# Latent attention: separate semaphores for the loads of QA and QB, and each query projected in slot 0 of a step

## What is computed

```python
B, T, C = (2, 512, 256); H, D = (16, 64); R = C // 8; ROPE = D // 2; NOPE = D - ROPE
q = (x @ Wq).reshape(b, t, H, D).transpose(0, 2, 1, 3)
ckv = x @ Wkva
kv_latent, k_rope = (ckv[:, :, :R], ckv[:, :, R:])
kv = (kv_latent @ Wkvb).reshape(b, t, H, NOPE).transpose(0, 2, 1, 3)
q = jnp.concatenate([q_nope, _rope(q_rope)], axis=-1)
k = jnp.concatenate([kv, _rope(k_rope)], axis=-1)
v = jnp.concatenate([kv, jnp.zeros_like(k_rope)], axis=-1)
att = jnp.einsum('bhqd,bhkd->bhqk', q, k) / jnp.sqrt(jnp.float32(D))
att = jax.nn.softmax(jnp.where(causal, att, -inf), axis=-1)
y = jnp.einsum('bhqk,bhkd->bhqd', att, v)
```

## Time and profile before

| what | value |
|---|---|
| median of 3 executions | 2580.61 us (2579.28 to 2582.89) |
| the profiled execution | 2586.34 us |
| its span (first to last instruction of the program) | 2584.6 us |
| stage of latent attention, steps 0 to 63 | 434.7 to 1490 us of the span |
| mean granted TensorE clock over the span | 0.965 |

### The profile page before, as it was taken

The page is one execution under the profiler, slowest core; times in us unless marked ns, Lnnn a source line. Parts: engine busy times, 40 slices in busy tenths (PEclk is TensorE's granted clock), DMA queues, the critical chain, the costliest instruction groups (busy, mean ns, idle before and its releaser), DMA issues. The chain is left out here.

```text
span 2584.6 us, 45266 instructions
## 1 busy us (share of the span) xinstructions
PE 2365.7 (92%) x16756; PEld 1955.3 (76%) x16756; DVE 1812.6 (70%) x3346; ACT 1340.9 (52%) x2031; POOL 930.2 (36%) x1042
## 2 busy tenths in 40 slices
PE   7998867999999999999999879999778888999999
PEld 5777655777777777777777768888667777888887
DVE  6888874787778777877787656666566657666564
ACT  5666543666666676667666643332234443333322
POOL 0323334364546464645444321121346641010000
PEclk8999987999999999999999979999889998999999
DMA  4011104433343334333433152332301113121221
GB/s 143 19 44 53 30 18 138 122 106 102 109 144 108 108 112 144 107 103 106 139 108 109 57 196 60 93 103 74 125 9 35 36 47 120 38 77 46 73 58 42
DMA packets 193179, 223.60 MB, mean 87 GB/s; under 512 B 37160, under 2 KB 156608, under 8 KB 189312
## 3 DMA queue, kind: packets, MB, share of 16 engines
q1 hardware_dynamic: 192960, 220.71, 29.3%
HBM read 150.75 MB, written 55.47 MB: 80 GB/s over the span
## 5 line engine op out<-in xcount | busy, mean ns | idle before, releaser
L1271 DVE TENSOR_REDUCE l_negmax<-l_mx 128x1 f32<-128x512 f32 (+3 forms) x608 | 390.8, 652 | 74.9 <-PE l_mx L1663 74.2
L1284 DVE TENSOR_TENSOR l_Plo<-l_s,l_Phi 128x512 fp32r<-128x512 f32 x576 | 368.8, 682 | 24.0 <-ACT l_s L1518 21.7
L1514 ACT ACTIVATE l_Phi<-l_s 128x1024 fp32r<-128x1024 f32 x288 | 293.7, 1020 | 136.3 <-PE l_s L1687 135.0
L1698 PE MATMUL l_o<-l_Phi,l_V 128*128 128x256 f32 x1152 | 301.6, 284 | 1.2 <-DVE l_Plo L1284 0.8
L1698 PE MATMUL l_o<-l_Plo,l_V 128*128 128x256 f32 x1152 | 299.4, 282 | 0.0
L1663 PE MATMUL l_mx<-l_KK,l_QA 128*128 128x512 f32 (+3 forms) x768 | 278.6, 402 | 20.7 <-DMA l_QB<-l_qd 11.2
L1518 ACT ACTIVATE l_s<-l_s 128x1024 f32<-128x1024 f32 x288 | 294.2, 1021 | 0.0
L2834 ACT ACTIVATE m_hidhi<-m_h 128x512 fp32r<-128x512 f32 x168 | 106.4, 633 | 355.5 <-DVE m_h L2683 355.5
L1685 PE MATMUL l_s<-l_QA,l_KK 128*128 128x512 f32 x576 | 257.6, 447 | 22.0 <-DVE l_Plo L1284 18.5
L1698 PEld LDWEIGHTS l_o<-l_Plo,l_V 128*128 128x128 f32 x1152 | 218.2, 189 | 16.1
L1687 PE MATMUL l_s<-l_QB,l_KL 65*128 65x512 f32 (+1 forms) x576 | 230.1, 399 | 0.0
(11 more groups left out here) (473 smaller groups left out, 6370.1 us busy)
## 6 DMA issues: line engine op xcount, KB each, us to landing
l_qd<-l_qs SPq DMA_DIRECT2D x256, 128.0 KB, 2.3
l_QA<-l_qd SPq DMA_DIRECT2D x64, 512.0 KB, 3.6
l_QB<-l_qd SPq DMA_DIRECT2D x64, 256.0 KB, 4.4
l_R<-l_rd SPq DMA_DIRECT2D x128, 128.0 KB, 2.9
m_spread<-m_combs SPq DMA_DIRECT2D x62, 256.0 KB, 5.2
m_spread<-m_combs SPq DMA_DIRECT2D x124, 128.0 KB, 4.9
xs<-next_store SPq DMA_DIRECT2D x32, 256.0 KB, 2.0
l_rps<-l_rp SPq DMA_DIRECT2D x128, 64.0 KB, 1.9
```

The source lines that it names most:

```text
L1271: v.tensor_reduce(negmax[:, n % 2, at + h0:at + h1], piece_of(number, chunk), AX.X, ALU.max, negate=True).then_inc(reduced, 1)
L1284: v.tensor_tensor(Plo[:, s % 3, x].rearrange("p h q -> p (h q)"), S2[s % 2][:, x * HALF:(x + 1) * HALF], Phi[:, s % 3, x].rearrange("p h q ...
L1514: a.activation(Phi[:, s % 3].rearrange("p u h q -> p (u h q)"), S2[s % 2][:, :], ACT.Exp, scale=L_D ** -0.5).then_inc(exped, 1)
L1698: mm = pe.matmul(O[:, odd * 2 * P:(odd + 1) * 2 * P].rearrange("p (j q) -> p j q", j=2), V[:, b % 2, k, 64 - 64 * odd:192 - 64 * odd], src ...
```

## The change

The semaphores `qready` become two sets, `aready` for the load of QA and `bready` for the load of QB. The first chunk of row maxima waits for `aready` alone; `score` waits for `bready` in the first unit of a step; `store_query` waits for both. And each piece of the work on a query moves one slot ahead: PE's `query` and ACT's `query_high` from slot 1 to 0, DVE's `query_low` from 2 to 1, POOL's `rope_queries` from 3 to 2. SP's order stays.

```diff
     def bank_work(self, m, i):
-        if i == 1 and self.asks(m + 3):
+        if i == 0 and self.asks(m + 3):
             yield "query", m + 3
...
                 if d >= 2:
-                    sp.wait_ge(qready[(d - 2) % 4], 32 * ((d - 2) // 4 + 1))
+                    sp.wait_ge(aready[(d - 2) % 4], 16 * ((d - 2) // 4 + 1))
+                    sp.wait_ge(bready[(d - 2) % 4], 16 * ((d - 2) // 4 + 1))
...
                 sp.dma_start(QA[:, d % 4].rearrange("p h t q -> p (h t q)").bitcast(F32),
-                             QD[d % 2].rearrange("c i h x -> (c i) (h x)")).then_inc(qready[d % 4], 16)
+                             QD[d % 2].rearrange("c i h x -> (c i) (h x)")).then_inc(aready[d % 4], 16)
                 sp.dma_start(QB[0:64, d % 4].rearrange("p h t q -> p (h t q)").bitcast(F32),
-                             QD[d % 2, 0:2].rearrange("c i h x -> (c i) (h x)"))\
-                    .then_inc(qready[d % 4], 16)
+                             QD[d % 2, 0:2].rearrange("c i h x -> (c i) (h x)")).then_inc(bready[d % 4], 16)
...
-                if i == 2 and L.asks(m + 3):
+                if i == 1 and L.asks(m + 3):
                     query_low(m + 3)
...
-                if i == 3 and L.asks(m + 3):
+                if i == 2 and L.asks(m + 3):
                     rope_queries(m + 3)
...
-                if i == 1 and L.asks(m + 3):
+                if i == 0 and L.asks(m + 3):
                     query_high(m + 3)
...
                 if number == L.before(n):
-                    pe.wait_ge(qready[n % 4], 32 * (n // 4 + 1))
+                    pe.wait_ge(aready[n % 4], 16 * (n // 4 + 1))
...
                 if u % UNITS == 0:
+                    pe.wait_ge(bready[m % 4], 16 * (m // 4 + 1))
                     pe.wait_ge(mready[m % 2], 32 * (m // 2 + 1))
...
-                if i == 1 and L.asks(m + 3):
+                if i == 0 and L.asks(m + 3):
                     query(m + 3)
```

More of the change, by code:

```diff
@@ L1039, in latent_attention @@
                                             for n in ("sstored", "sready", "rstored", "rready"))
-        qready = [signal(f"qready{i}") for i in range(4)]
+        aready, bready = ([signal(f"{n}{i}") for i in range(4)] for n in ("aready", "bready"))
         block = ctx.enter_context(nc.Block())
```

## The result

| | median of the runs | against the kernel before | interval (95%) |
|---|---|---|---|
| before, beside it | 2581.75 us (2579.28 to 2584.17, 4 executions) | | |
| the changed kernel | 2618.96 us (2618.41 to 2622.46, 4 executions) | 1.0136 | 1.0118 to 1.0154 |

The change makes the kernel slower by 1.4%, some 35 us. The prediction said slower, 2600 us with a range to 2614; the time lies 5 us above that range. The profiled execution took 2618.41 us.

What follows compares the result with a forecast made beforehand. The prediction took PE as the bound, with 52 us idle in the stage. Its terms, -6.5 - 1 + 6 + 17 + 4 = +19.5 us, on the median of 2580.6 gave 2600 us, range 2584 to 2614.

Steps and rivals of the forecast that it cites:

- Part 1: Row maxima wait for QA alone: 9.7 of 11.2 us of waits go, two thirds reach the end, -6.5 us.
- part 4: PE's granted clock falls behind the six stalls, counted in half to all: +4 us, bounds 0 and +10.
- The idle time before the weight loads: Alternative count for the QA wait: 21.5 us of weight loads' waits for QB, making that term about -12.5 us.
- Part 2: Query one slot earlier on DVE: query_low stands for ACT's copy in odd steps, +6 us; even steps -1 us.
- The -1 of the even steps: About 0.5 us gained in steps 14, 30 and 46, where ACT was late, with small things: -1 us.
- Part 3: On POOL inverse_root stands behind rope_queries, so DVE and PE stall in six steps: +17 us, bounds +10 and +20.5.
- rival (b): Clock falls in every stall (+10), odd steps pay more often (+12), POOL's 20.5: 2616 us; chance 0.14.
- rival (c): Load wait goes in full, neither order costs since the rope ends before inverse_root matters: 2572 us; chance 0.06.
- (a): DVE's stall mostly covered, 1.3 us for each of the six, no fall of the clock: 2587 us; chance 0.15.
- (d): QA itself comes too late, bound by the same store; the wait merely takes its name: 2607 us; chance 0.03.

Runs made afterwards that it cites:

- e2: The kernel before with the two separate semaphore sets alone, all query work in its old slots; 2577.24 us, ratio 0.9977.
- e1: The changed kernel with POOL's inverse_root put back ahead of rope_queries, both in slot 2; 2586.76 us, ratio 1.0019.
- e5: e1 with DVE's query_low back in slot 2 in odd steps; 2583.65 us, ratio 1.0009.
- e12: e6 with PE's query in slot 0 in odd steps too; 2584.2 us, ratio 1.0002.
- e6: e2 with the query one slot early on PE, ACT and DVE in even steps alone, POOL's rope in slot 3; 2572.39 us, ratio 0.9972.
- e9: The kernel before with six more reductions on DVE ahead of normalize or rms in six steps; 2611.43 us, ratio 1.0109.
- e11: The kernel before with two more reductions on DVE ahead of normalize or rms in six steps; 2592.16 us, ratio 1.0034.
- e10: The changed kernel with one more power of 128x8 on POOL ahead of inverse_root's own; 2627.52 us, ratio 1.0175.
- e7: The changed kernel with QB's load issued behind the next query's row swap instead of ahead of it; 2605.24 us, ratio 1.0096.

## Why the prediction was right in direction and short in size

- **Part 1, the wait for QA: right in its mechanism and near in size.** -6.5 us forecast, 6 measured (e2), and the part that comes back shows as waits for l_Plo. That the two numbers meet so closely is luck: some 3 us of the gain by e2's trace are step 3, with its clock, and the forecast counted the clock of step 3 elsewhere (part 4). The idle time before the weight loads, which the rule of the Trainium skill named in the prediction (Perfetto Trace Analysis, Identifying the Most-Contended Engine) would have counted, gave -12.5; e2's interval is a gain of 3.4 to 8.8 us, so here the matmuls' own wait was the one to count.
- **Part 2, the odd steps: mechanism wrong, term too small.** e1 less e2 is 0.42%, 11 us (give or take 4), where the parts' sum was -1 + 6 = +5. I read in step 29 what waits behind `query_low` and took the low end of my bounds; the amounts per step that I gave (15 steps of 0.3 to 1.0 us, 15 of 0 to 0.3) have their middle at 12 us, near the 11 measured, though the reason was another. Putting `query_low` back gave 2 us (e5); PE's query in slot 0 of the odd steps costs 7.7 us by itself (e12 against e6). The cost was PE's order: with the query in slot 0 DVE has, by the reading above, nothing to reduce. I had only written that PE's work in slots 0 to 4 is the same and so skipped the engine that feeds DVE. The -1 of the even steps is not contradicted (e6 less e2, -1.3 us give or take 4), and too small to be shown.
- **Part 3, POOL's order: right in its chain, and nearly in size.** Six waits of 3.4 us forecast, 3.7 measured on average (22.1 in all). PE's idle time for it is 17.4 us by the traces of the changed kernel and e1, for the +17 of the sum. Two small errors nearly cancel: the swap took 3.5 us in step 40 where I carried over 2.6, as it now comes 1.7 us behind QB's load, which lengthened the waits; and 4.7 us of them came back where I took off 3.5.
- **Part 4, the clock: the step that failed, and it had no reason for its size.** It reads "Six stalls of over 3 us invite the same. I count it in half to all of them, +4 us"; PE's busy time rose by 9.9 us against e1 and 9.2 against before. The earlier trace rows showed a fall of the clock after 2.2 us of idle time, so six stalls of 3.7 us gave no reason to count it in half. 10 was my upper bound. The Trainium skill (TensorE: Matmul & The Clock Gate, HAM oscillation — how this bites in real kernels) puts the penalty at half of the time spent at the lower clock. The six windows of the changed kernel hold 37 us of it (their lengths times one less the clock, doubled), which makes 19 us, as an estimate by that rule; measured are 9 to 10. Part of the gap is that PE stood still for 9 of some 38 us at the lower clock (busy 28.8) and had nothing to lose then; the rest is open.
- **The sum.** -6.5 + 5 + 21 = +19.5 was forecast; e2, e1 less e2, and the changed kernel less e1 give -6 + 11 + 30 = +35. The gap is 6 us of part 2 and 9 of parts 3 and 4. The corrections have the size of those of rival (b), at 2616 with a chance of 0.14, which was priced too low. It had the clock right; its +12 for the odd steps is right in number alone, as it rests on `query_low`. Its 2616 also lies outside the range that was said to hold over half of it, and the -8.5 of rival (c) is nowhere worked out. The profiled execution of before also lay 5.7 us above the median on which I put the sum, and that of the changed kernel did not, so part of the miss is in what the sum was put on.
- Rivals (a), (c) and (d) fell: of 22.1 us of stalls only 4.7 came back, no rope ended in time, and QA's wait is 1.5 us.

## What to carry to other kernels

Before moving work by a slot on an in-order engine, list what else that engine runs in the slot that it moves into: here two instructions of together 2 us, six times put behind one that waits for a DMA, cost 30 us of 2580. A stall of the bound's feeder is priced twice, once as idle time and once in the lower clock behind it, so count the second in full for stalls like these (3.6 us on DVE; at 1.2 us it came in three steps of six). And order the loads on a queue by who needs them first: QB's load behind the swap was worth 10 us (give or take 7) in the changed kernel and 8 (give or take 5) in e6.

## What the runs showed of the hardware that I had not expected

- The length of a stall of DVE doesn't by itself say whether the granted clock falls: six added stalls of about 1.2 us (two reductions, by e9's 3.64 us for six) brought it down in three steps and left it at 1.00 in three (e11). And with one more power of 1.75 us in each of the six stalls the clock stayed down for longer (about 48 us in all for 37), at no more PE busy time (e10, 1012.46 and 1012.41 us).
- An exchange of two transfers of 64 KB, issued 1.7 us behind a 256 KB load, let the instruction that waits for it start 3.5 us after its issue, 0.9 us later than one issued 3.3 us behind that load, or ahead of it (step 40 of the changed kernel, of before and of e7).
